# High halves by casting transfers from GpSimd's queue in a fused post-norm decoder layer on one core

## The reference

```
q = silu(x @ Wq1 @ Wq2); a = exp(log_sigmoid(sigmoid(x @ Wk1 @ Wk2)))
v = x @ Wv; h[t] = a[t]*h[t-1] + (1-a[t])*v[t]      # 512 channels, over the tokens
out = q*h; out = out * rsqrt(mean(out*out) + 1e-6) * norm_w
x = layernorm(x + out @ Wo)
x = layernorm(x + attention(x, ctx, ctx))            # 8 heads, softmax over 256
x = layernorm(x + (silu(x @ Wg.T) * (x @ Wu.T)) @ Wd.T)   # 1024 hidden
```

## Time and profile before

| what | us |
|---|---|
| median of 3 runs | 172.11 (171.77 to 173.91) |
| the profiled execution | 171.14 |
| its span, first to last instruction | 169.1 |
| around the span | 2.04 |
| TensorE busy | 157.0 |
| GpSimd busy | 75.0 |

### The profile page before, as it was taken

One profiled execution on the slowest core, in us unless ns is written; L12 is line 12 of the kernel. 1 busy time (PEld: TensorE's weight loads), 2 busy tenths in 40 slices (PEclk: granted clock), 3 DMA queues, 4 the chain that ended last, 5 costly groups with the idle time before them and its releaser, 6 DMA issues.

```text
span 169.1 us, 4296 instructions
## 1 busy us (share of the span) xinstructions
PE 157.0 (93%) x1722; PEld 139.3 (82%) x1722; DVE 116.6 (69%) x225; ACT 88.6 (52%) x146; POOL 75.0 (44%) x106
## 2 busy tenths in 40 slices
PE   6998898989899999999999999999998999899970
PEld 2787797877677999997899999779897789799970
DVE  2559869978978994997967585596757473444753
ACT  3678898889598455287336037612616504115300
POOL 3069499897906560333386236152203317025302
PEclk9999999999999999999999999999999999999998
DMA  5999394002042000000200100000010000000101
GB/s 179 315 402 390 63 342 173 6 2 62 4 124 68 0 4 0 0 4 0 66 0 6 62 4 0 0 4 0 4 62 2 4 0 4 0 0 0 66 0 62
DMA packets 5155, 10.50 MB, mean 62 GB/s; under 512 B 656, under 2 KB 1680, under 8 KB 5136
## 3 DMA queue, kind: packets, MB, share of 16 engines
q1 hardware_dynamic: 4992, 9.97, 17.0%
q10 hardware_dynamic: 144, 0.26, 0.5%
HBM read 9.18 MB, written 1.05 MB: 60 GB/s over the span
## 4 chain that ended last, share of the span: by engine, by line
PE 76%; DVE 4%; issue 1%; ACT 1%; POOLq 0%; POOL 0%; DVEq 0%
PE banks L428 41%; PE banks L642 9%; PE banks L592 4%; PE banks L647 4%; PE banks L604 4%; PE banks L575 3%; PE banks L547 3%; DVE banks L946 1%; PE banks L536 1%; PE banks L569 1%; PE banks L580 1%; PE banks L557 1%; PE banks L614 1%; PE banks L504 1%; ACT top_rows L760 1%
## 5 line engine op out<-in xcount | busy, mean ns | idle before, releaser
L1128 POOL TENSOR_TENSOR g_lo<-gu,g_hi 128x512 fp32r<-128x512 f32 x15 | 19.8, 1322 | 38.5 <-ACT g_hi L808 38.5
L800 ACT ACTIVATE gu<-banks 128x512 f32<-128x512 f32 x16 | 9.6, 598 | 27.9 <-PE banks L428 27.9
L946 DVE TENSOR_REDUCE banks<-banks 128x4 f32<-128x1024 f32 x16 | 19.6, 1228 | 5.7 <-PE banks L547 4.2
L991 DVE SCALAR_TENSOR_TENSOR gu<-gu,banks 128x512 f32<-128x512 f32 x16 | 11.0, 686 | 16.7 <-ACT gu L800 16.7
L770 ACT ACTIVATE prob<-banks 128x1024 f32<-128x1024 f32 x16 | 15.6, 1024 | 6.3 <-PE banks L580 6.3
L642 PE MATMUL banks<-w_down_hi,g_hi 128*128 128x256 f32 x64 | 16.1, 283 | 0.0
L642 PE MATMUL banks<-w_down_lo,g_hi 128*128 128x256 f32 x64 | 15.8, 280 | 0.0
L428 PE MATMUL banks<-x2t_hi,w_gate_hi 128*128 128x256 f32 x64 | 13.9, 298 | 0.8 <-ACT x2t_hi L791 0.8
L777 ACT ACTIVATE res<-banks,shift,rstd 128x256 f32<-128x256 f32 x16 | 8.2, 563 | 10.9 <-POOL shift L1113 10.9
L428 PE MATMUL banks<-x2t_lo,w_gate_hi 128*128 128x256 f32 x64 | 13.0, 284 | 0.0
L808 ACT ACTIVATE g_hi<-gu 128x512 fp32r<-128x512 f32 x16 | 10.0, 631 | 5.7 <-DVE gu L994 5.7
(11 more groups left out here) (143 smaller groups left out, 439.7 us busy)
## 6 DMA issues: line engine op xcount, KB each, us to landing
prob<-w_ffn SPq DMA_DIRECT2D x4, 512.0 KB, 5.8
spare<-w_ffn SPq DMA_DIRECT2D x2, 512.0 KB, 7.9
ctx_raw<-ctx SPq DMA_DIRECT2D x4, 256.0 KB, 5.4
ctx_t<-ctxT SPq DMA_DIRECT2D x4, 256.0 KB, 4.5
res<-x SPq DMA_DIRECT2D x4, 256.0 KB, 4.4
prob<-w SPq DMA_DIRECT2D x3, 256.0 KB, 4.4
res<-xT SPq DMA_DIRECT2D x3, 256.0 KB, 6.8
out<-res SPq DMA_DIRECT2D x3, 256.0 KB, 2.2
```

The costliest lines, as they stand in the source:

```text
L800: nc.scalar.activation(gu[:, n % 2, :].rearrange("p (k t) -> p k t", k=2), place["gate", b, i][:, :, :], ACT.Tanh, scale=0.5).then_inc(gta ...
L946: nc.vector.tensor_reduce(neg_top(b, t)[:, 4 * k:4 * k + 4], place["scores", b, i][:, :, :], AX_X, ALU.max, negate=True).then_inc(top_done, 1)
L991: nc.vector.scalar_tensor_tensor(out=v, in0=v, scalar=1.0, in1=place["gate", b, i][:, :, :], op0=ALU.add, op1=ALU.mult).then_inc(gate_done, 1)
L1128: nc.gpsimd.tensor_tensor(g[1][:, 2 * i:2 * i + 2, :], gu[:, n % 2, :].rearrange("p (k t) -> p k t", k=2), g[0][:, 2 * i:2 * i + 2, :], AL ...
```

## The change

ScalarE's twelve copies at line 682 go. In their place twelve transfers, issued from GpSimd's queue, read the same arrays from memory once more and round them on the way into the high half. The raw arrays are still loaded as before, since the low half needs them; the engine that subtracts now waits for both transfers.

```diff
+            def cast_xt_high(b, i):
+                if b >= WHOLE + 2:
+                    pool.wait_ge(value_done, 2 * (b - 1))
+                    pool.wait_ge(low_done, 2 * (b - 1))
+                pool.dma_start(xt[0][:, b % 2, :, :].rearrange("p c t -> p (c t)"), xT[b]).then_inc(cast_xt[b], 16)
+            def cast_w_high(b, i):
+                pool.dma_start(w_high[0][:, 1 - i, :], w2[:, (1 - i) * C:(2 - i) * C]).then_inc(cast_high[i], 16)
+            def cast_w_v(b, i):
+                pool.dma_start(w_v[0][:, :, :].rearrange("p c n -> p (c n)"), wv).then_inc(cast_v, 16)
+            def cast_w_ffn(b, i):
+                pool.dma_start(ffn_chunk(i, 0, 4)[0], w_ffn[:, i, :]).then_inc(cast_ffn[i], 16)
...
             def ffn_rest(b, i):
-                pool.wait_ge(ffn_w_hi, i // 2 + 1)
+                pool.wait_ge(cast_ffn[i // 2], 16)
+                pool.wait_ge(in_ffn[i // 2], 16)
...
             def split_xt(b, i):
-                dve.wait_ge(xt_hi, b + 1 - WHOLE)
+                dve.wait_ge(cast_xt[b], 16)
+                dve.wait_ge(in_xt[b], 16)
...
             def w_high_rest(b, i):
-                dve.wait_ge(high_w_hi, i + 1)
+                dve.wait_ge(cast_high[i], 16)
+                dve.wait_ge(in_high[i], 16)
...
             def low_proj(b, i):
-                pe.wait_ge(xt_hi, b + 1 - WHOLE)
+                pe.wait_ge(cast_xt[b], 16)
```

`xt_rest`, `w_v_rest`, `value_proj` and `high_proj` change their waits in the same way. `PLAN` and `BANKS` are new as a whole. Two lines of `PLAN`:

```diff
+    "pool.cast_ffn": [[7.22, 8.22, 9.22, 24.11, 28.02, 30.34]],
-    "pool.ctx": [[], [15.1], [59.05], [90.44]],
+    "pool.ctx": [[], [43.15], [70.78], [87.98]],
```

More of the change, by code:

```diff
@@ L57 @@
     "sp.w_low": [[0.7]],
-    "sp.xt": [[], [1.2], [4.2], [5.7]],
-    "sp.w_high": [[1.7, 3.7]],
-    "sp.w_v": [[2.2]],
+    "sp.w_high": [[1.2, 3.7]],
+    "sp.w_v": [[1.7]],
+    "sp.xt": [[], [2.2], [4.2], [4.7]],
     "sp.w_o": [[2.7]],
[L62 to L80, removed]
@@ L81 @@
-    "act.load_xt": [[0.7]],
[L82 to L96, removed]
@@ L105 @@
[L105 to L111, removed]
@@ new lines @@
+    "sp.ctx": [[5.7], [6.7], [46.25], [46.75]],
+    "sp.weights": [[6.2, 7.2, 8.2, 19.65, 20.15, 23.47]],
+    "sp.x": [[11.8], [12.3], [16.9], [47.25]],
+    "sp.store": [[94.44], [120.46], [155.82], [163.24, 164.37]],
+    "pe.low": [[4.03, 4.89], [9.15, 14.96], [17.18, 23.24], [40.59, 48.14]],
+    "pe.decay": [[5.74, 6.59], [11.58, 14.25], [23.94, 27.48], [46.02, 52.58]],
+    "pe.value": [[7.45, 9.86], [15.76, 17.88], [26.07, 30.74], [53.29, 60.04]],
+    "pe.query": [[12.54, 13.39], [24.65, 25.36], [38.21, 41.3], [70.73, 71.67]],
@@ new lines @@
+    "pe.squares": [[19.3], [32.76], [54.71], [86.32]],
+    "pe.mixed": [[19.82], [33.28], [55.23], [87.51]],
+    "pe.scores": [[29.51, 39.54], [47.36, 64.29], [78.07, 97.05], [109.45, 121.23]],
+    "pe.turn_top": [[36.11, 43.74], [58.06, 71.44], [87.28, 101.04], [115.89, 125.22]],
+    "pe.shifted": [[37.04, 44.86], [59.0, 72.39], [90.34, 101.97], [116.83, 126.16]],
+    "pe.sums": [[48.98], [76.27], [105.84], [130.03]],
+    "pe.context": [[50.78], [78.85], [107.65], [131.83]],
+    "pe.turn_x": [[58.52], [86.84], [116.13], [142.13]],
@@ new lines @@
+    "pool.cast_ffn": [[7.22, 8.22, 9.22, 24.11, 28.02, 30.34]],
+    "pool.wo": [[10.22]],
+    "pool.xt": [[], [], [15.53], [37.61]],
+    "pool.weights": [[16.84, 18.16, 19.47, 20.79, 25.11, 29.02, 33.97, 35.29, 38.93, 40.24, 45.18, 46.49]],
+    "pool.rms": [[22.1], [36.6], [57.22], [90.01]],
+    "pool.norm1": [[26.43], [41.56], [60.97], [93.3]],
+    "pool.outputs": [[], [31.34, 32.66], [50.29, 51.61], [85.35, 86.67]],
+    "pool.ctx": [[], [43.15], [70.78], [87.98]],
+    "pool.norm2": [[55.62], [83.76], [112.62], [137.87]],
@@ L138 @@
-    "turn_top": [[5, 0], [4, 7], [3, 7], [4, 2]],
-    "shifted": [[4, 6, 2, 4], [4, 2, 6, 4], [0, 4, 2, 6], [4, 2, 2, 6]],
-    "sums": [[7], [3], [6], [6]],
-    "context": [[0], [2], [7], [1]],
-    "turn_x": [[0], [2], [7], [3]],
-    "gate": [[0, 2, 6, 2], [2, 1, 4, 1], [0, 4, 1, 0], [1, 3, 6, 7]],
-    "up": [[6, 3, 2, 1], [0, 6, 5, 0], [1, 5, 0, 7], [0, 7, 5, 3]],
-    "down": [[6], [6], [2], [4, 0]],
+    "low": [[0, 1], [3, 1], [6, 4], [2, 3]],
+    "decay": [[0, 1], [5, 4], [3, 0], [2, 2]],
@@ new lines @@
+    "value": [[2, 4], [0, 7], [1, 5], [0, 5]],
+    "query": [[3, 2], [6, 5], [7, 3], [2, 4]],
+    "squares": [[5], [0], [2], [2]],
+    "mixed": [[2], [6], [4], [0]],
+    "scores": [[2, 6, 4, 0], [6, 4, 4, 6], [0, 6, 0, 4], [2, 0, 4, 0]],
+    "turn_top": [[7, 4], [5, 1], [4, 0], [2, 4]],
+    "shifted": [[0, 2, 4, 0], [0, 6, 6, 0], [2, 6, 0, 4], [0, 4, 4, 0]],
+    "sums": [[0], [2], [4], [0]],
+    "context": [[1], [3], [7], [3]],
+    "turn_x": [[2], [3], [3], [5]],
+    "gate": [[3, 2, 0, 3], [4, 6, 2, 7], [2, 6, 7, 6], [3, 5, 0, 7]],
```

112 lines of the change are left out of this document (55 added, 57 removed).

## The result

The changed kernel takes 177.65 us (median of 4 runs, 177.22 to 178.22), where the kernel before took 172.9 us in the same comparison: a ratio of 1.033 with an interval of 1.029 to 1.038. It is slower. The profiled execution took 177.68 us, its span is 175.8 us, so it stands for the median.

What follows compares the result with a forecast made beforehand. TensorE, without slack, and GpSimd until sums 0 were taken as the bounds, with the DMA full early. GpSimd's later row adds 3.9 us to 171.14, 175.0, plus 0.97 for the median: 176.0 us, range 172.5 to 181.5.

Steps and rivals of the forecast that it cites:

- The DMA: Early loads: 27 units through full engines, so the first feed-forward chunk lands at 22.0 us; share near 1 until about 23.
- rival B: Casting transfers run at half the rate of plain ones: 183.9 us; chance 0.13 for it or something between.
- the two queues share equally or go in order of issue: DMA queues of the early loads: equal shares assumed, 27 units, 21.05 us; in order of issue 26 units, 0.6 us less.
- The issue on GpSimd: Each cast issue holds GpSimd 1.0 us, bounds 0.43 and 1.29; eight at the start free, four in its gapless row.
- rival A: A cast's issue holds GpSimd for next to nothing: 172.8 us; chance 0.22.
- Place 1, scores 0.0: TensorE's scores 0.0 wait for norm1 0 until 33.9 us, against 30.30; TensorE 2.2 us behind there.
- Place 2, exp 0.3 behind GpSimd: GpSimd's row ends at 52.0 us, exp 0.3 starts then, sums 0 at 53.2: 3.9 us lost.
- The first delay lies inside the second: Delays at scores 0.0 and sums 0 overlap, so the sum is not 6.1 but 3.9 us.
- waits that hang on VectorE: TensorE idle at places that depend on VectorE: not costed, named as a sign that the forecast is wrong.
- The sign that I had named for a right forecast: Profile page after the change: TensorE shows 3 to 4 us more idle time with the same busy time.
- ScalarE's relief at nothing: ScalarE's 10.5 us of removed copies count as no gain, since TensorE hardly waits for ScalarE.
- Rival C: ScalarE's relief wins: both TensorE waits of rows 2 go, -2.5 us, 169.6 us; chance 0.05.

Runs made afterwards that it cites:

- the late casts: Kernel before, old order, with casts of xT, w_high, w_v and feed-forward chunks 3 to 5 (from 24 us), ScalarE copying chunks 0 to 2: 177.13 us, 1.032.
- The run with the early root: Changed kernel with GpSimd's four gate-weight subtractions put behind norm1 0: 181.83 us, ratio 1.059 to the kernel before.
- The run with the filled wait: Changed kernel plus 20 unread matmuls in a free bank ahead of TensorE's wait before scores 0.0: 176.77 us, ratio 1.025 to the kernel before.

## Why the prediction was right in size and half right in cause

The forecast was 176.0 us in a range of 172.5 to 181.5, and slower. It came out at 177.65 us, 4.8 above the kernel before in the same comparison, where I had added 3.9. Step by step:

**The DMA: right.** The first chunk was forecast to land at 22.0 us, by counting 27 units at the rate of the rows; GpSimd started on it at 22.34. The share near 1 held until 28 us, longer than the 23 I named. Casts at the rate of plain transfers: right, rival B is out. Whether the two queues share equally or go in order of issue is not shown: the sums for the two differ by 0.6 us, and the same load released GpSimd at 22.34 us here, at 22.00 and at 21.44 us in the two runs with 20 more matmuls.

**The issue on GpSimd: a term of the wrong size.** I took 1.0 us with bounds of 0.43 and 1.29, and it is 0.54 to 0.63. The eight issues ended at 6.8 us, not 10.4, Wo landed at 11.0, not 13. The row from the first chunk to the last `w_down_lo` took 28.4 us, not 30.0; four issues at 0.6 in place of 1.0 are 1.6 of it. Yet rival A, in which such issues cost next to nothing, is not right either: in the late casts the place of three of them decided 3.3 us.

The Trainium skill (DMA: Bandwidth & Descriptors, section Anatomy of one DMA — SWDGE (gpsimd) path) calls the descriptor generation small and variable. That speaks for rival A, 172.8 us. The trace agrees as far as 0.55 us of GpSimd is small beside the 5 to 13 us from issue to landing; in a row without a gap it is not small.

**Place 1, scores 0.0: right, with one link missed.** 33.9 us predicted, 33.72 measured, and so 2.0 us behind where I had 2.2. What I had not seen is that VectorE's list is held too. Mixed 0.0 waited 3.55 us for the root, silu 1.0 stood behind it, and scores 0.0 needed the bank that silu 1.0 frees; that came last, at 33.51, level with norm1 at 33.45. I had also not followed x of batch 0 through the full DMA: it landed at about 27.4 us, a microsecond before the root was there. The run with the early root shows that this alone would have held the place. And the casts aren't all of it: in the new order TensorE comes to mixed 0.0 only at 22.60 us, not 18.60, and with the order alone scores 0.0 come at 32.84 us, behind a wait of 1.48 us.

**Place 2, exp 0.3 behind GpSimd: failed.** The whole sum of 3.9 us came from this place, on the ground that "The first delay lies inside the second". GpSimd's row ended at 50.71, not 52.0, and exp 0.2 was still waiting for TensorE, until 51.79. The first delay did not shrink on the way to sums 0; it grew from 2.0 to 5.5 us, by two terms that the prediction did not have:

- the clock, 1.6 us of longer matmuls. TensorE stood idle for 2.5 us and then had matmuls at 0.55 of full speed. The run with the filled wait shows that at full clock 0.5 of it would be another wait, so about 1.0 us is the clock's alone.
- the gap ahead of turn_top 0.1, 1.59 in place of 0.19 us. In the new order only low 3.0 and query 2.1 stand between scores 0.1 and turn_top 0.1, and VectorE's two maxima of 1.23 us each take longer than these. The order alone has the same 1.59 us without a cast. The prediction listed waits that hang on VectorE as what it had not costed.

2.0 + 1.6 + 1.4 = 5.0 of the 5.5 us. So the forecast came close by luck: it put the loss at a place that doesn't bind, and left out the two terms that make up more than half of it. The sign that I had named for a right forecast fails in the same way: not 3 to 4 us more idle time with the same busy time, but 4.9 us and 1.8 us more busy time.

**ScalarE's relief at nothing: not contradicted.** ScalarE has twelve copies less (busy 79.7 in place of 88.6 us), TensorE still waits 1.1 us for `top_rows`, and every experiment with casts is slower than before. Rival C is out; no run shows what the relief alone is worth.

**What the casts' cost is made of.** In the old order twelve casts cost 1.024. Less early traffic alone does not lower it (1.033); with three issues moved behind the low half as well it is 1.026, and with three casts fewer 1.013. The earliest six units alone cost 1.007. The traces show three ways in which the time is lost: raw loads, ctx and x late by the traffic, issues in GpSimd's row ahead of what TensorE needs, and a lower clock behind a wait of TensorE. For the second and third a run shows what they are worth: moving three issues won 1.9%, filling the wait about 1.0 us. The first was taken away in the runs with casts later, but there the second took its place. What is not settled is how the 3.3% of the change divide between the casts and the new order. The order cost 0.9% beside all casts, 1.2% beside few and 2.8% or more with none, and in that last run copies placed by hand held GpSimd as the DMA does in the changed kernel.

## What to carry to other kernels

A transfer that replaces a copy on an engine with slack can be paid three times: in bandwidth while the raw loads are due, in the issuing engine's row, and in what lands late behind it. Change the order in a run of its own, with nothing else, or its cost can't be told from that of the transfers. Follow every load that is issued into the full stretch, the last ones too, to its user. And where a step on the path waits, ask whether the wait is long enough for the matrix engine's clock to fall: here a wait of 2.5 us was followed by matmuls that took 1.6 us longer.
